# Edge stage of a graph network: padded operands, one compare, merged products, and an addition moved to POOL

## The chip, the cores and the metric

The kernel runs on one core of one Trainium2 chip. The metric is the device time of one execution in microseconds (us).

## What is computed

A block with three parts works on 6250 nodes of 256 features: a graph network over 200,000 edges, linear attention, and a mixture of eight experts. The change lies in the edges of the graph network alone. `g0` (64 scalars) and `g1` (64 vectors of 3) are the features of an edge's source node, `y0` and `y1` are four attributes of the edge, and `wa` to `wd` are weights that a small network makes from ten further attributes:

```python
h = silu(edge_length_embedded @ W_mlp1 / math.sqrt(N_BASIS))
ew = h @ W_mlp2 / math.sqrt(N_HID)
g0 = f0[edge_src]; g1 = f1[edge_src]
m0a = wa * g0 * y0[:, None]
m0b = wb * einsum('eum,em->eu', g1, y1) / math.sqrt(3.0)
m1a = wc[:, :, None] * g0[:, :, None] * y1[:, None, :]
m1b = wd[:, :, None] * g1 * y0[:, None, None]
s_mid = segment_sum(concatenate([m0a, m0b], 1), edge_dst)
v_mid = segment_sum(concatenate([m1a, m1b], 1), edge_dst)
```

The edges come sorted by destination.

## The kernel before

The program has six stages, one behind the other: `prepare`, `nodes`, `edges`, `update`, `dispatch` and `experts`. The stage of the change, `edges`, works through NI = 440 items. An item is a group of 512 edges (GE = 512, held as GC = 4 chunks of 128 edges, one edge per partition) seen against one block of 128 destination nodes. A group whose edges reach into a second block comes again as a further item. Each engine has a loop of its own over the items, unrolled four times, and semaphores tie the loops together. In the text, messages(n) stands for the messages of item n, and so on. For item n:

- SyncE (L657 to L671) waits until messages(n-4) and hot_y(n-4) are done (L661, L662; both counters start at FREE = 4), reads the group's number (L663), and issues six loads: `src`, `dst`, `y` (L665 to L667), and the ten edge attributes three times as high and low parts into 30 rows of `el` (L670).
- POOL (L673 to L683) waits for messages(n-4) and for the loads of n (L677, through `wait_apart`, L82), and then issues four indirect transfers (L679) that gather the 128 source rows of each chunk from a table in memory into `rows`.
- TensorE (L778 to L817) computes in `body`: `weights(n)`, the second layer of the small network in fp32 (L791); `hidden(n+1)`, its first layer with 30 rows against 512 columns (L785); and `sums(n-1)`, eight fp32 products (L802) that sum the messages by destination, with the one-hot matrices `hot_y` and `hot` as weights.
- ACT (L685 to L709) applies silu (L689), makes the vector part of `Z` from g0 and y1 in twelve activations (L696), and scales `hot` by y0 to `hot_y` in four (L703).
- DVE (L711 to L776) rebases the destinations (`rel`, L731), multiplies g1 by y1 (`dot3`, L736), compares with a ramp to get the one-hot matrices (`hot`, L742), adds two of the three parts of the dot product (`dot2`, L745) and later the third (L763, into the scalar part of `Z`), and multiplies `rows` and `Z` with the weights in four products (L754 and L758, each twice). The last of them, `scalars(1, Z[h])`, counts up `messages`. Then `flush(n-1)` (L724) adds the sums of the item before to the accumulators.

`src`, `dst`, `y`, `el` and `rows` have four buffers each; `rel`, `hot`, `hot_y`, `Z`, `dot3`, `dot2`, `msg`, `hT` and the PSUM tiles have two. No scheduler decides an order: every engine works through what its loop says, in that order.

## Time and profile before

| what | value |
|---|---|
| median of 3 runs | 3996.39 us (3994.59 to 3999.0) |
| span of the profiled execution | 3989.3 us |
| mean granted TensorE clock | 0.978 |
| busy: PE, DVE, ACT, POOL | 97%, 72%, 65%, 64% |
| edge stage, first gather to last flush | 274.47 to 2832.36 us |

The time of the profiled execution itself is not listed beside its span; the median of the runs is 7.1 us above the span. Busy time is work of an engine and leaves waits out. The same tile name `k_x` stands for everything that lies in the large buffer `K.x2` during this stage: `rows`, `Z`, `msg`, and, before the change, `dot3` and `dot2`. A gather is an instruction of POOL (about 1 us, in which its transfer is described) and a transfer that lands later.

### The profile page before, as it was taken

To read this page: it belongs to the slowest core of one execution; us is meant where nothing else is said; L and a number is where in the kernel's file an instruction comes from. 1 tells how busy PE (TensorE), PEld (TensorE's weight loads), DVE (VectorE), ACT (ScalarE), POOL (GpSimd) and SP (SyncE) were. 2 spreads that over 40 slices of the span, in tenths; PEclk is the share of its full clock that TensorE was granted. 3 is DMA by queue.
4 is the path that set the end of the run, shared out by engine and by line. 5 is a ranking of instruction groups with operands and counts; after the bars stand their busy time and mean duration, and the time that the engine had idled before them with its cause. 6 is when DMAs were issued, how large, how long until landed. Compare 5 with 4: busy or idle time off the path is not lost. (4 is left out here: it accounts for less than half of the span.)

```text
span 3989.3 us, 81744 instructions
## 1 busy us (share of the span) xinstructions
PE 3852.3 (97%) x18082; PEld 3206.0 (80%) x18082; DVE 2881.2 (72%) x5613; ACT 2595.5 (65%) x8731; POOL 2544.3 (64%) x2339
## 2 busy tenths in 40 slices
PE   6979999999999999999999999999997699999998
PEld 5868888888888888878887888788896588888887
DVE  7769999999999999999999999999666600000000
ACT  6668887888788778877887788778424233333332
POOL 5647777777777777777777777777311344444443
PEclk9989999999999999999999999999995899999999
DMA  7863333433333333434334334333222366666665
GB/s 224 257 194 103 102 103 103 104 103 104 103 104 103 104 103 104 104 103 104 104 103 104 103 104 104 104 103 104 75 79 87 104 186 194 193 193 193 194 193 151
DMA packets 436225, 509.01 MB, mean 128 GB/s; under 512 B 254375, under 2 KB 345355, under 8 KB 421851
## 3 DMA queue, kind: packets, MB, share of 16 engines
q0 software_dynamic: 109904, 273.02, 24.5%
q1 hardware_dynamic: 326283, 235.54, 20.7%
q8 instruction: 17, 0.28, 0.0%
q14 instruction: 21, 0.17, 0.0%
HBM read 444.92 MB, written 63.33 MB: 127 GB/s over the span
## 5 line engine op out<-in xcount | busy, mean ns | idle before, releaser
L679 POOL DMA_INDIRECT k_x<-gather_table,edges_src x1760 | 1996.8, 1135 | 557.4 <-issue 447.6
L696 ACT ACTIVATE k_x<-k_x,edges_y 128x64 f32<-128x64 f32 x5280 | 1303.5, 336 | 4.2 <-DMA k_x<-gather_table,edges_src 4.0
L802 PE MATMUL edges_ps_sum<-k_x,edges_hot_y 128*128 128x256 f32 x3520 | 1093.6, 392 | 0.5 <-issue 0.5
L802 PE MATMUL edges_ps_sum<-k_x,edges_hot 128*128 128x256 f32 x3520 | 1047.6, 379 | 0.0
L703 ACT ACTIVATE edges_hot_y<-edges_hot,edges_y 128x128 f32<-128x128 f32 x1760 | 562.7, 390 | 505.6 <-DVE edges_hot L742 505.6
L791 PE MATMUL edges_ps_edge<-k_w_e,edges_hT 100*128 100x256 f32 x3520 | 836.4, 380 | 7.8 <-ACT edges_hT L689 7.8
L758 DVE TENSOR_TENSOR k_x<-k_x,edges_ps_edge 128x768 f32<-128x768 f32 x880 | 794.6, 942 | 0.0
L802 PEld LDWEIGHTS edges_ps_sum<-k_x,edges_hot_y 128*128 128x128 f32 x3520 | 633.0, 190 | 175.5 <-issue 107.1
L791 PEld LDWEIGHTS edges_ps_edge<-k_w_e,edges_hT 100*128 100x128 f32 x3520 | 670.5, 191 | 101.7 <-issue 7.6
L802 PEld LDWEIGHTS edges_ps_sum<-k_x,edges_hot 128*128 128x128 f32 x3520 | 669.4, 190 | 91.3
L1407 DVE TENSOR_TENSOR experts_raw<-experts_ps_y,experts_b 128x256 f32<-128x256 f32 x112 | 42.4, 420 | 725.6 <-PE experts_ps_y L1363 725.6
L1317 POOL DMA_INDIRECT out<-experts_y,experts_idx_out x112 | 178.4, 1593 | 423.4 <-issue 386.6
L724 DVE TENSOR_TENSOR accumulators<-accumulators,edges_ps_sum 128x512 f32 x440 | 302.7, 688 | 171.7 <-PE edges_ps_sum L802 164.3
L736 DVE TENSOR_TENSOR k_x<-k_x,edges_y 128x768 f32<-128x768 f32 x440 | 419.4, 953 | 0.0
L1353 PE MATMUL experts_ps_h<-experts_xT,experts_w 128*128 128x256 f32 x1792 | 397.7, 380 | 1.7 <-ACT experts_xT L1381 1.6
L1363 PE MATMUL experts_ps_y<-experts_w,experts_hT 128*128 128x256 f32 x1792 | 396.0, 379 | 0.0
L1390 ACT ACTIVATE experts_hT<-experts_ps_h,experts_constants 128x256 f32<-128x256 f32 x448 | 212.5, 474 | 271.2 <-PE experts_ps_h L1353 271.2
L1353 PEld LDWEIGHTS experts_ps_h<-experts_xT,experts_w 128*128 128x128 f32 x1792 | 341.3, 191 | 49.5 <-ACT experts_xT L1381 1.9
L1363 PEld LDWEIGHTS experts_ps_y<-experts_w,experts_hT 128*128 128x128 f32 x1792 | 336.2, 190 | 43.4
L754 DVE TENSOR_TENSOR k_x<-k_x,edges_ps_edge 128x256 f32<-128x256 f32 x880 | 362.3, 412 | 1.6 <-PE edges_ps_edge L791 1.6
L742 DVE TENSOR_TENSOR edges_hot<-k_iota_f,edges_rel 128x512 f32<-128x512 f32 x440 | 301.3, 685 | 0.0
L1381 ACT ACTIVATE experts_xT<-experts_ps_x,experts_constants 128x256 f32<-128x256 f32 x112 | 57.2, 560 | 313.3 <-DMA experts_w<-in_w 313.3
(248 smaller groups left out, 3508.8 us busy)
## 6 DMA issues: line engine op xcount, KB each, us to landing
experts_w<-in_w SPq DMA_DIRECT2D x112, 1024.0 KB
k_x<-gather_table,edges_src POOLq DMA_INDIRECT x1760
edges_el<-el_hi SPq DMA_DIRECT2D x880, 20.0 KB
edges_el<-el_lo SPq DMA_DIRECT2D x440, 20.0 KB
nodes_el<-in_el SPq DMA_DIRECT2D x46, 170.0 KB, 3.6
el_hi<-nodes_el_hi SPq DMA_DIRECT2D x46, 170.0 KB
el_lo<-nodes_el_lo SPq DMA_DIRECT2D x46, 170.0 KB
experts_b<-in_b SPq DMA_DIRECT2D x56, 128.0 KB
```

The lines of the kernel that those rows point to most:

```text
L679: nc.gpsimd.indirect_dma_start(out=rows[k][:, j, :], out_offset=None, in_=K.table_d.rearrange("t p d -> (t p) d"), in_offset=bass.Indirect ...
L696: x = nc.scalar.activation(Z[k % 2][:, j, MUL * (i + 1):MUL * (i + 2)], rows[k][:, j, 0:MUL], ACT.Identity, scale=y[k][:, j, 1 + i:2 + i])
L703: x = nc.scalar.activation(hot_y[k % 2][:, j, :], hot[k % 2][:, j, :], ACT.Identity, scale=y[k][:, j, 0:1])
L724: v.tensor_tensor(a, a, ps_s[k % 2][:, :], ALU.add).then_inc(c["flushed"], 1)
L736: v.tensor_tensor(dot3[h][:, :, :, :], rows[k][:, :, MUL:D].rearrange("p c (i u) -> p c i u", i=3), y[k][:, :, 1:4].unsqueeze(3).to_broadc ...
L742: v.tensor_tensor(hot[h][:, :, :], K.iota_f[:, :].unsqueeze(1).to_broadcast([P, GC, P]), rel[h][:, :].unsqueeze(2).to_broadcast([P, GC, P] ...
L754: return v.tensor_tensor(msg[h][:, :, o * D:o * D + MUL], factor[:, :, 0:MUL], w[:, :, o * P:o * P + MUL], ALU.mult)
L758: return v.tensor_tensor(three(msg[h][:, :, o * D + MUL:(o + 1) * D]), three(factor[:, :, MUL:D]), spread(w[:, :, o * P + MUL:(o + 1) * P] ...
L791: x = t.matmul(ps_e[k % 2][:, j * 256:(j + 1) * 256], hT[k % 2][:, j * P:(j + 1) * P], K.w_e2[:, :], start=True, stop=True)
L802: x = t.matmul(into[:, :, o, :], rows_hot[k % 2][:, j, :], msg[k % 2][:, j, o * D:(o + 1) * D], start=j == 0 and o == 0, stop=j == GC - 1, ...
L1353: x = t.matmul(ps_h[j % 4][:, 0:SB], w1[k][:, h, j * P:(j + 1) * P], xT[k][:, h, :], start=h == 0, stop=h == 1)
L1363: x = t.matmul(ps_y[s][:, 0:D], hT[k][:, j, s * P:(s + 1) * P], w2[k][:, j, :], start=j == 0, stop=j == NH - 1)
```

## The change

All of it lies in `edges`, apart from the size and clearing of one weight tile:

- `el` gets 128 partitions instead of 30, cleared once by POOL, and `w_e1s` likewise (SyncE waits for the clearing before its first load). The hidden layer's matmul then has 128 rows, 98 of them zero.
- The rebasing and the compare become one instruction, which reads the integer destinations itself: (ramp + base) == dst. The ramp and `K.item_base` are as they were.
- `rows` and `Z` lie side by side in `both`, so that the four products become two: one of 8 x 192 columns for all vectors, and one of 8 x 64 for all scalars, which now comes last and counts up `messages`.
- `Z` and `hot` get four buffers; `dot3` and `dot2` get one, in the attention's weight tile, which is free in this stage.
- The last addition of the dot product (`third`) leaves DVE for POOL. POOL's loop for item n issues the gathers of item n and then `third(n-3)`. DVE waits for it (`dot`) ahead of the last product.
- DVE flushes item n-2 between `before(n)` and `after(n)`, where it flushed n-1 at the end of n.
- ACT's wait for messages ahead of `Z` is gone, and its wait ahead of `hot_y` goes by `summed`.

```diff
@@ prepare, POOL and DVE
+            g.memset(K.w_e1s[:, :].bitcast(f32), 0.0)
...
-            nc.vector.tensor_copy(K.w_e1s[:, :], w_part[:, :]).then_inc(scaled, 1)
+            nc.vector.tensor_copy(K.w_e1s[0:3 * BAS, :], w_part[:, :]).then_inc(scaled, 1)
@@ edges, buffers
-    FREE = 4
+    FREE, AHEAD = 4, 2
...
-        el, src, dst = four("el", [3 * BAS, GE], f32r), four("src", [P, GC], i32), four("dst", [P, GC], i32)
+        el, src, dst = four("el", [P, GE], f32r), four("src", [P, GC], i32), four("dst", [P, GC], i32)
...
+        both, msg = [cut(2 * k) for k in range(4)], [cut(8 + 2 * k) for k in range(2)]
+        rows, Z = ([b[:, :, o * D:(o + 1) * D] for b in both] for o in range(2))
@@ edges, SyncE
+            sp.wait_ge(c["padded"], 4)
+
             def body(n, k):

                 sp.wait_ge(c["messages"], n + 1)
@@ edges, POOL
+            for k in range(4):
+                nc.gpsimd.memset(el[k][:, :].bitcast(f32), 0.0).then_inc(c["padded"], 1)
+
             def body(n, k):

                 wait_apart(pool, c["passed"], (c["messages"], n + 1), (loaded[k], per(n, k, LD, 4)))
...
-            steps(pool, NI, 4, 0, body)
+                if not (isinstance(n, int) and n < 3):
+                    third(n - 3, (k - 3) % 4)
+
+            def third(n, k):
+                wait_apart(pool, c["passed"], (c["dot2"], n + 1))
+                nc.gpsimd.tensor_tensor(Z[k][:, :, 0:MUL], dot2[:, :, :], dot3[:, :, 2, :], ALU.add).then_inc(c["dot"], 1)
+            steps(pool, NI, 4, 4, body)
+            for n in range(NI - 3, NI):
+                third(n, n % 4)
@@ edges, ACT
-                act.wait_ge(c["messages"], n + 3)
...
-                act.wait_ge(c["flushed"], n + 1)
+                act.wait_ge(c["summed"], n + 1)
@@ edges, DVE
-                dve.wait_ge(c["hot"], n)
-                v.tensor_scalar(rel[h][:, :], dst[k][:, :], K.item_base[:, bass.ds(n, 1)], None,
-                                ALU.subtract).then_inc(c["rel"], 1)
+                dve.wait_ge(c["flushed"], n + 1)
+                v.scalar_tensor_tensor(hot[k][:, :, :], K.iota_f[:, :].unsqueeze(1).to_broadcast([P, GC, P]),
+                                       K.item_base[:, bass.ds(n, 1)], dst[k][:, :].unsqueeze(2).to_broadcast([P, GC, P]),
+                                       ALU.add, ALU.is_equal).then_inc(c["hot"], 1)
...
-                v.tensor_tensor(hot[h][:, :, :], K.iota_f[:, :].unsqueeze(1).to_broadcast([P, GC, P]),
-                                rel[h][:, :].unsqueeze(2).to_broadcast([P, GC, P]), ALU.is_equal).then_inc(c["hot"], 1)
...
-                v.tensor_tensor(Z[h][:, :, 0:MUL], dot2[h][:, :, :], dot3[h][:, :, 2, :], ALU.add).then_inc(c["dot"], 1)
-                vectors(0, rows[k])
                 dve.wait_ge(c["factors"], n + 1)
-                vectors(1, Z[h])
-                dve.wait_ge(c["dot"], n + 1)
-                scalars(1, Z[h]).then_inc(c["messages"], 1)
+                v.tensor_tensor(three(g[:, :, MUL:D]), three(f[:, :, MUL:D]),
+                                w[:, :, MUL:P].unsqueeze(2).to_broadcast([P, 2 * GC, 3, MUL]), ALU.mult)
+                dve.wait_ge(c["dot"], n + 1)
+                v.tensor_tensor(g[:, :, 0:MUL], f[:, :, 0:MUL], w[:, :, 0:MUL], ALU.mult).then_inc(c["messages"], 1)
...
+            def body(n, k):
+                before(n, k)
+                flush(n - 2, (k - 2) % 4)
+                after(n, k)
@@ edges, TensorE
-                pe.wait_ge(c["flushed"], n + 1)
+                pe.wait_ge(c["flushed"], n + 3)
```

The order of instructions on POOL, before the change, in the loop over the items (`L679 DMA` is a gather, the register and ISA rows are counters and waits):

```order
L56 ISA
L85 ISA
L679 DMA k_x<-gather_table,edges_src 128x256 x4
L85 REGISTER_ALU
L679 DMA k_x<-gather_table,edges_src 128x256 x4
L85 REGISTER_ALU
L679 DMA k_x<-gather_table,edges_src 128x256 x8
L56 REGISTER_ALU
L56 COMPARE_AND_BRANCH
```

And in the changed kernel, whose lines stand a few further down (L687 is the gather, L696 is `third`, whose operands `dot2` and `dot3` lie in `k_w_kvT`):

```order
L687 DMA k_x<-gather_table,edges_src 128x256 x4
L85 REGISTER_ALU
L696 TENSOR_TENSOR k_x<-k_w_kvT 128x4x64
L85 REGISTER_ALU
L687 DMA k_x<-gather_table,edges_src 128x256 x4
L85 REGISTER_ALU
L696 TENSOR_TENSOR k_x<-k_w_kvT 128x4x64
```

An addition now stands behind every four gathers; it belongs to the item three before the one that is gathered.

On DVE, before, one item from the rebasing to the last product:

```order
L731 TENSOR_SCALAR edges_rel<-edges_dst,k_item_base 128x4
L736 TENSOR_TENSOR k_x<-k_x,edges_y 128x4x192
L742 TENSOR_TENSOR edges_hot<-k_iota_f,edges_rel 128x512
L745 TENSOR_TENSOR k_x<-k_x 128x4x64
L754 TENSOR_TENSOR k_x<-k_x,edges_ps_edge 128x4x64
L762 REGISTER_ALU
L763 TENSOR_TENSOR k_x<-k_x 128x4x64
L758 TENSOR_TENSOR k_x<-k_x,edges_ps_edge 128x4x192 x2
L754 TENSOR_TENSOR k_x<-k_x,edges_ps_edge 128x4x64
```

And in the changed kernel (L745 is the compare, L739 the flush, L767 and L770 the merged products):

```order
L745 SCALAR_TENSOR_TENSOR edges_hot<-k_iota_f,k_item_base,edges_dst 128x512
L749 REGISTER_ALU
L751 TENSOR_TENSOR k_w_kvT<-k_x,edges_y 128x768
L735 REGISTER_ALU
L735 TENSOR_LOAD k_item_block
L735 ISA x2
L736 REGISTER_ALU
L739 ISA
L739 TENSOR_TENSOR accumulators<-accumulators,edges_ps_sum 128x512
L758 TENSOR_TENSOR k_w_kvT<-k_w_kvT 128x256
L767 TENSOR_TENSOR k_x<-k_x,edges_ps_edge 128x8x192
L770 TENSOR_TENSOR k_x<-k_x,edges_ps_edge 128x8x64
```

The flush moved up between the first product and the first addition, the second addition is gone from DVE, and the product that completes the messages is the last instruction of the item as before.

## Rows read from the trace of the kernel before

**Rows 1.** The page, part 1: busy us (share of the span) and instructions.

```profile
PE 3852.3 (97%) x18082; PEld 3206.0 (80%) x18082; DVE 2881.2 (72%) x5613; ACT 2595.5 (65%) x8731; POOL 2544.3 (64%) x2339
```

**Rows 2.** A stretch: us, busy of PE, PEld, DVE, ACT, POOL, clock, DMA share, GB/s.

```profile
1100.00:1600.00 500.00, 500.00 (x2164) 400.69 (x2163) 467.57 (x867) 399.46 (x1470) 393.84 (x347) 1.00 0.40 104
```

**Rows 3.** Order of time on PE, one item: start us, duration us, engine, line.

```profile
1504.09 1.89 PE L791 MATMUL edges_ps_edge<-k_w_e,edges_hT 100*128 100x256 f32 x8
1505.91 0.47 PE L785 MATMUL edges_ps_hidden<-edges_el,k_w_e1s 30*100 30x512 f32 x1
1506.32 0.70 PE L802 MATMUL edges_ps_sum<-k_x,edges_hot_y 128*128 128x256 f32 x2
1506.85 0.59 PE L802 MATMUL edges_ps_sum<-k_x,edges_hot 128*128 128x256 f32 x2
...
1509.87 1.89 PE L791 MATMUL edges_ps_edge<-k_w_e,edges_hT 100*128 100x256 f32 x8
```

**Rows 4.** Order of time on DVE, one item; in brackets idle time before.

```profile
1503.68 0.41 DVE L754 TENSOR_TENSOR k_x<-k_x,edges_ps_edge 128x256 f32<-128x256 f32 x1
1504.47 0.69 DVE L724 TENSOR_TENSOR accumulators<-accumulators,edges_ps_sum 128x512 f32 x1 [0.38 <-PE edges_ps_sum L802]
...
1505.21 0.95 DVE L736 TENSOR_TENSOR k_x<-k_x,edges_y 128x768 f32<-128x768 f32 x1
1506.08 0.69 DVE L742 TENSOR_TENSOR edges_hot<-k_iota_f,edges_rel 128x512 f32<-128x512 f32 x1
1506.68 0.42 DVE L745 TENSOR_TENSOR k_x<-k_x 128x256 f32<-128x256 f32 x1
...
1507.72 1.81 DVE L758 TENSOR_TENSOR k_x<-k_x,edges_ps_edge 128x768 f32<-128x768 f32 x2
```

**Rows 5.** Order of time on POOL, one item.

```profile
1505.51 1.53 POOL L679 DMA_INDIRECT k_x<-gather_table,edges_src  x1 [0.30 <-issue]
1507.35 1.01 POOL L679 DMA_INDIRECT k_x<-gather_table,edges_src  x1 [0.30 <-DMA edges_el<-el_lo]
```

**Rows 6.** Waits of SyncE: queue and line, waited for, us in total, times, longest.

```profile
SPq L663 <- DVE k_x L754: 750.2, 436, 2.4
```

**Rows 7.** Order of time on SyncE: the first load of an item.

```profile
1505.19 0.36 SPq L665 DMA_DIRECT2D edges_src<-in_src  x1
```

**Rows 8.** Start of the edge stage on SyncE.

```profile
269.63 0.35 SPq L665 DMA_DIRECT2D edges_src<-in_src  x1
```

**Rows 9.** Start of the edge stage on POOL.

```profile
274.47 1.07 POOL L679 DMA_INDIRECT k_x<-gather_table,edges_src  x1 [11.35 <-DMA edges_el<-el_hi]
...
278.48 1.01 POOL L679 DMA_INDIRECT k_x<-gather_table,edges_src  x1 [0.30 <-issue]
```

**Rows 10.** Order of time on POOL in the node stage.

```profile
131.18 1.01 POOL L398 DMA_INDIRECT nodes_dst<-in_dst_rows,first_groups_i  x1 [0.30 <-issue]
132.21 0.74 POOL L420 TENSOR_TENSOR nodes_q<-nodes_q_high,nodes_q_low 128x256 f32<-128x256 f32 x1
```

**Rows 11.** PE at the stage's start, with the granted clock at 0.50.

```profile
286.57 3.78 PE L791 MATMUL edges_ps_edge<-k_w_e,edges_hT 100*128 100x256 f32 x8 [0.69 <-ACT edges_hT L689]
290.29 0.74 PE L785 MATMUL edges_ps_hidden<-edges_el,k_w_e1s 30*100 30x512 f32 x1
290.96 1.22 PE L802 MATMUL edges_ps_sum<-k_x,edges_hot_y 128*128 128x256 f32 x2
291.97 1.06 PE L802 MATMUL edges_ps_sum<-k_x,edges_hot 128*128 128x256 f32 x2
```

**Rows 12.** The same stretch: us, busy of each engine, clock.

```profile
285.00:294.00 9.00, 8.31 (x18) 5.51 (x18) 7.57 (x14) 5.82 (x21) 7.06 (x7) 0.50 0.39 105
```

**Rows 13.** A memset of POOL (groups by line: busy us, mean ns).

```profile
L160 POOL MEMSET k_zeros<- 128x512 f32 x1 | 0.5, 537 | 0.0
```

**Rows 14.** DVE: end of the first item, and the last flush.

```profile
287.65 0.41 DVE L754 TENSOR_TENSOR k_x<-k_x,edges_ps_edge 128x256 f32<-128x256 f32 x1
...
2831.67 0.69 DVE L724 TENSOR_TENSOR accumulators<-accumulators,edges_ps_sum 128x512 f32 x1 [3.41 <-PE edges_ps_sum L802]
```

More of the change, by code:

```diff
@@ L638, in edges @@
         two = lambda name, shape, dt=f32: [m.sb(f"{name}{k}", shape, dt) for k in range(2)]
-        el, src, dst = four("el", [3 * BAS, GE], f32r), four("src", [P, GC], i32), four("dst", [P, GC], i32)
-        y = four("y", [P, GC, 4])
-        rel, hT = two("rel", [P, GC]), two("hT", [HID, GE])
-        hot, hot_y = two("hot", [P, GC, P]), two("hot_y", [P, GC, P])
+        el, src, dst = four("el", [P, GE], f32r), four("src", [P, GC], i32), four("dst", [P, GC], i32)
+        y, hT = four("y", [P, GC, 4]), two("hT", [HID, GE])
+        hot, hot_y = four("hot", [P, GC, P]), two("hot_y", [P, GC, P])
+        spare = K.w_kvT[:, :, :].rearrange("p c n -> p (c n)")
+        dot3 = spare[:, 0:3 * GC * MUL].rearrange("p (c i u) -> p c i u", c=GC, i=3)
+        dot2 = spare[:, 3 * GC * MUL:].rearrange("p (c u) -> p c u", c=GC)
         warm = m.sb("warm", [P, 1])
         room = K.x2[:, :, :].rearrange("p t d -> p (t d)")
-        cut = lambda at, n: room[:, at * GC * D:(at + n) * GC * D].rearrange("p (c n) -> p c n", c=GC)
-        rows, Z, msg = [cut(k, 1) for k in range(4)], [cut(4 + k, 1) for k in range(2)], [cut(6 + 2 * k, 2) for k in range(2)]
-        dot3 = [cut(10 + k, 1)[:, :, 0:3 * MUL].rearrange("p c (i u) -> p c i u", i=3) for k in range(2)]
-        dot2 = [cut(10 + k, 1)[:, :, 3 * MUL:] for k in range(2)]
+        cut = lambda at: room[:, at * GC * D:(at + 2) * GC * D].rearrange("p (c n) -> p c n", c=GC)
+        both, msg = [cut(2 * k) for k in range(4)], [cut(8 + 2 * k) for k in range(2)]
+        rows, Z = ([b[:, :, o * D:(o + 1) * D] for b in both] for o in range(2))
         ps_e = [m.ps(f"edge{k}", 2) for k in range(2)]
@@ L651, in edges @@
         loaded, gathered = ([m.sem(f"{x}{k}") for k in range(4)] for x in ("loaded", "gathered"))
-        c = {x: m.sem(x) for x in ("cleared", "messages", "flushed", "hidden", "act", "weights", "factors", "rel", "hot_y",
+        c = {x: m.sem(x) for x in ("padded", "cleared", "messages", "flushed", "hidden", "act", "weights", "factors", "hot_y",
                                    "dot3", "dot2", "dot", "hot", "summed", "passed")}
@@ L692, in body @@
                 act.wait_ge(gathered[k], per(n, k, 64, 4))
-                act.wait_ge(c["messages"], n + 3)
                 for j in range(GC):
                     for i in range(3):
-                        x = nc.scalar.activation(Z[k % 2][:, j, MUL * (i + 1):MUL * (i + 2)], rows[k][:, j, 0:MUL],
+                        x = nc.scalar.activation(Z[k][:, j, MUL * (i + 1):MUL * (i + 2)], rows[k][:, j, 0:MUL],
                                                  ACT.Identity, scale=y[k][:, j, 1 + i:2 + i])
@@ L700, in body @@
                 act.wait_ge(c["hot"], n + 1)
-                act.wait_ge(c["flushed"], n + 1)
+                act.wait_ge(c["summed"], n + 1)
                 for j in range(GC):
-                    x = nc.scalar.activation(hot_y[k % 2][:, j, :], hot[k % 2][:, j, :], ACT.Identity, scale=y[k][:, j, 0:1])
+                    x = nc.scalar.activation(hot_y[k % 2][:, j, :], hot[k][:, j, :], ACT.Identity, scale=y[k][:, j, 0:1])
                 x.then_inc(c["hot_y"], 1)
@@ L746, in body @@
                                 ALU.add).then_inc(c["dot2"], 1)
+                eight = lambda a: a.rearrange("p c (o n) -> p (c o) n", o=2)
+                w = ps_e[h][:, :].rearrange("p (g n) -> p g n", g=2 * GC)
+                three = lambda a: a.rearrange("p g (i u) -> p g i u", i=3)
+                f, g = eight(both[k]), eight(msg[h])
                 dve.wait_ge(c["weights"], n + 1)
-                w = ps_e[h][:, :].rearrange("p (c n) -> p c n", c=GC)
-                three = lambda a: a.rearrange("p c (i u) -> p c i u", i=3)
@@ L751, in body @@
-                spread = lambda a: a.unsqueeze(2).to_broadcast([P, GC, 3, MUL])
-                def scalars(o, factor):
-                    return v.tensor_tensor(msg[h][:, :, o * D:o * D + MUL], factor[:, :, 0:MUL],
-                                           w[:, :, o * P:o * P + MUL], ALU.mult)
-                def vectors(o, factor):
-                    return v.tensor_tensor(three(msg[h][:, :, o * D + MUL:(o + 1) * D]), three(factor[:, :, MUL:D]),
-                                           spread(w[:, :, o * P + MUL:(o + 1) * P]), ALU.mult)
@@ L778, in _ @@
+            for n in range(2):
+                before(n, n)
+                after(n, n)
+            steps_from(dve, 2, NI, 4, body)
+            for n in (NI - 2, NI - 1):
+                flush(n, n % 4)
         @block.tensor
@@ L800, in sums @@
                 for j in range(GC):
-                    for o, rows_hot in ((0, hot_y), (1, hot)):
-                        x = t.matmul(into[:, :, o, :], rows_hot[k % 2][:, j, :], msg[k % 2][:, j, o * D:(o + 1) * D],
+                    for o, rows_hot in ((0, hot_y[k % 2]), (1, hot[k])):
+                        x = t.matmul(into[:, :, o, :], rows_hot[:, j, :], msg[k % 2][:, j, o * D:(o + 1) * D],
                                      start=j == 0 and o == 0, stop=j == GC - 1, skip_group_check=True)
```

29 lines of the change are left out of this document (10 added, 19 removed).

## The prediction

> **What bounds the kernel now.** I read the busy shares first, then the stretches, then one item of the edge stage on each engine, then its start. TensorE is busy 97% of the span [rows 1], and in the middle of the edge stage 500.00 us of 500 at the full clock (1.00, which is the 2.4 GHz level) [rows 2]. An item takes 5.78 us there: the first weight-network product starts at 1504.09 and the next item's at 1509.87 [rows 3]. So TensorE sets the pace, and its 440 items, 5.78 each, are some 2540 us of the 3989.
>
> The other engines have room. DVE waits 0.38 us for the sums before each flush and works for the other 5.40 [rows 4]. POOL starts four gathers per item 1.31 us apart, 5.25 us in all, and the last 0.53 of its period is a gather that lasts 1.53 instead of 1.01 [rows 5]. The loads have slack of another kind, which matters below. SyncE waits at L663, 436 times, for the DVE product L754 that completes an item's messages [rows 6]. That product ends at 1503.68 + 0.41 = 1504.09, and the first load of item n+4 is issued at 1505.19 [rows 4, 7]. What then follows (loads, gathers, the item's work) may take four items, 23.1 us, since there are four buffers. A long latency is hidden by this depth, and a part of the chain that loses the depth would show it in full.
>
> **The change, part by part.**
>
> *DVE.* It loses the rebasing (L731), one addition (L763) and the start-up of two merged products. From the end of one item's messages to the wait for `dot` it has the compare (0.69), the product (0.95), the flush (0.69), the first addition (0.42) and the vectors' product (1.81) [rows 4]: 4.6 us at most. Whatever the merged forms and the integer operand of the compare cost (between nothing and a doubling of the compare, 0.69) lies under the wait that I find next, which leaves DVE idle for some 7 us.
>
> *TensorE.* Padding the hidden layer from 30 to 128 rows leaves 512 columns. Today the hidden layer costs 0.41 us from its start to the next matmul, the product behind it 0.53 where the seven others take (1509.87 - 1506.85) / 7 = 0.43 each, and the four products ahead of it 1.82 where four times 0.43 is 1.73 [rows 3]. (A product of 256 columns in fp32 shows as two records, x2.) The part that padding could remove is between nothing and 0.41 + 0.10 + 0.09 - 0.22 = 0.38 us, with 0.22, one record's share of 0.43, as the least that a matmul here takes. The Trainium skill (TensorE: Matmul & The Clock Gate, Step-by-step: what each phase is for) says that loading weights takes time by columns and that the number of rows does not matter; by that the padding would give nothing, unless its other statement, that a load is only pulled ahead when row groups do not conflict, is what the 30-row tile runs into. The sum below does not depend on it.
>
> *POOL.* This is the term that decides. The addition that completes Z (L763) moves to POOL as `third(n-3)`, and it stands there behind the four gathers of item n. POOL works in order. Those gathers wait for the loads of item n, and SyncE issues these only when the messages of item n-4 are done. Shift the index by one and follow it round: messages(n-1) are complete; SyncE may load item n+3; POOL may gather item n+3; only then comes `third(n)`; only then can DVE make the last product of item n, which completes messages(n). The step from one item's messages to the next now contains a whole load, four gathers, the addition and a product. The four-deep buffers no longer help, because the chain passes from n-1 to n, not from n-4 to n. Its price:
>
> - messages to the first load's issue: 1505.19 - 1504.09 = 1.10 us [rows 4, 7];
> - first issue to the start of the first gather: at the stage's start, where POOL was waiting, 274.47 - 269.63 = 4.84 us [rows 8, 9]. With gathers of the item before still in flight it can be longer. Bounds: 4.5, and 5.8 (one microsecond more). I take 5.0, near the row;
> - four gathers with POOL otherwise idle: from 274.47 to 278.48 + 1.01 = 279.49, that is 5.02 us [rows 9];
> - the addition behind a gather: the same form starts 0.02 us after a gather's end and takes 0.74 [rows 10]; with 0.05 for the semaphore (an estimate; ACT's and SyncE's starts behind DVE's ends are of this size) 0.81 us;
> - the last product, now 128x512 from PSUM: the flush of that size takes 0.69 [rows 4].
>
> Together 1.10 + 5.00 + 5.02 + 0.81 + 0.69 = 12.62 us per item, where 5.78 was. Bounds 12.1 to 13.4.
>
> Does anything else reach that length? DVE's other work, 4.6 us, does not. ACT's does not: it fits in 5.78 today. TensorE is now busy for 5.4 to 5.8 us in 12.6, and its clock may fall. When it was at 0.50, the 1.2 GHz level, the second layer's four products took 290.29 - 286.57 = 3.72, the hidden layer 0.67, and the first of the sums 1.01; seven more at twice 0.43 make 11.4 us per item [rows 11, 12]. That is still under 12.62, and it runs beside the chain: sums(n-1), weights(n+1) and hidden(n+2) all lie between messages(n-1) and messages(n). So the clock costs nothing, with about a microsecond to spare.
>
> *How many items.* Loads 4 to 439 wait for messages 0 to 435, and each then holds back the addition three items behind: messages 1 to 436, so 436 rounds: 436 x 12.62 = 5502 us.
>
> *Ends of the stage.* Before the first load POOL now clears four 128x512 tiles, 4 x 0.54 [rows 13] = 2.1 us. messages(0) then need all sixteen first gathers: 274.47 + 2.1 + 15 x 1.31 + 1.01, some 0.8 for collisions with DVE, the addition 0.81 and the product 0.69 give 299.6; before, they were done at 288.06 [rows 14]. Behind messages(436) three items remain without loads, some 15 us, then the last sums (8 x 0.43 = 3.5) and a flush (0.7): 19 us. The stage ends at 299.6 + 5502 + 19 = 5820.6 instead of 2831.67 + 0.69 = 2832.4 [rows 14]. Nothing behind it changes. The difference is +2988 us on the profiled span of 3989.3. The median of the runs, 3996.4, lies 7.1 above that span, and I keep this distance: 3996.4 + 2988 = 6984, say **6985 us**.
>
> **The rivals.**
>
> *1. TensorE stays the bound (ends faster).* If POOL's order did not hold the addition back, the stage would keep TensorE's pace and win what padding gives, 0 to 0.38 us x 440 = 0 to 167 us: 3830 to 3996, middle 3915. For it: TensorE has no gap at all today, and the four engines' busy times all fit in 5.8 us. Against it: it needs the load of item n+3 to be issued before messages(n-1), and SyncE is seen to wait exactly there [rows 6]; or the addition to overtake gathers. It decides for this rival only if the round costs less than 5.8 us, and the four gathers and the addition alone are 5.8. Chance 3%.
>
> *2. POOL's own work becomes the bound, without the round.* Four gathers at 1.31, the addition 0.76, and collisions. The long gather shows what these are: it starts at 1505.51, inside DVE's product of two SBUF operands (L736, from 1505.21, next start 1506.08), and lasts 1.53 instead of 1.01; 1506.08 is also where the extra 0.52 ends [rows 4, 5]. The addition reads two SBUF operands and could be held up the same way, and hold up DVE. With one or two such losses POOL needs 6.2 to 6.9 us per item: (6.5 - 5.78) x 440 = +320, so 4315 us. The Trainium skill (SBUF — State Buffer, SBUF: two separate sides) calls this an exclusive lock between GpSimd and a DVE operation with two SBUF inputs; the trace agrees, by the 0.52. Against this rival: DVE is idle while POOL gathers and adds in the round, so the two would seldom meet. Chance 2%.
>
> *3. The round without the load.* If loads were early and only the gathers' wait for messages mattered, the round would be 0.9 + 5.02 + 0.81 + 0.69 = 7.4 us, (7.4 - 5.78) x 436 = +707: 4700 us. Against it stands SyncE's wait again. Chance 2%.
>
> *4. The round, and TensorE's low clock as the bound.* If at 1.2 GHz an item costs over 12.6 us (11.4 from the rows, plus waits of its own order), the stage goes by TensorE: at 13.5 us per item +3370, so 7365 us. It decides from 1.2 us more than the rows show. Chance 3%.
>
> **How the numbers follow.** The forecast has the remaining 90%. Its time is 6985. Its own range comes from the round's bounds: 12.1 gives 436 x 0.52 = 227 less, and 13.4 gives 340 more. 6800 to 7300 holds most of that (some nine parts in ten), about 81% of all; the rivals are left out. A measurement of this kernel can tell 0.2% (8 us) from no change. Rival 1's 3% splits into faster, 2%, and within 0.2%, 1%, where padding gives next to nothing; slower has 97%.
>
> **What would show it.** In the changed profile, one item should take about 12.6 us in the middle of the edge stage, and TensorE's busy share there should fall to 45% at full clock or up to 90% at half. The wait that ends DVE's scalar product should be POOL's addition. POOL should be idle for about 6 us per item, released by a load of `edges_el`, then run four gathers and the addition without a gap. SyncE's wait for DVE's messages should be far more than half of its time. If one item takes 6 to 7 us, rival 2 or 3 was right; if TensorE shows no idle time, rival 1 or 4. If DVE shows more than 5 us of work per item, the compare with an integer operand is dearer than I bound it, without effect on the time.

## The result and the profile after

| | before | changed |
|---|---|---|
| median of 4 runs | 3996.95 us | 6861.47 us (6859.99 to 6865.73) |
| ratio, 95% interval | 1 | 1.7171 (1.7147 to 1.7196) |
| profiled span | 3989.3 us | 6859.2 us |
| mean granted TensorE clock | 0.978 | 0.811 |

The forecast was 6985 us, within 6800 to 7300. Some 2865 us went into the edge stage and nowhere else of note. Part 1 of the page of the changed kernel, and two of its groups (busy us, mean ns, idle time of the engine before them and who ended it):

```profile
PE 4754.9 (69%) x18082; PEld 3888.0 (57%) x18082; DVE 2623.3 (38%) x3853; ACT 2595.5 (38%) x8731; POOL 2659.9 (39%) x2784
...
L770 DVE TENSOR_TENSOR k_x<-k_x,edges_ps_edge 128x512 f32<-128x512 f32 x440 | 302.6, 688 | 3286.7 <-POOL k_x L696 3286.7
...
L745 DVE SCALAR_TENSOR_TENSOR edges_hot<-k_iota_f,k_item_base,edges_dst 128x512 f32<-128x512 f32 x440 | 328.2, 746 | 0.0
```

No engine is near its limit any more. The last product of an item, L770, has 3286.7 us of idle time before it, all of it ended by POOL's L696, the addition that moved. In the middle of the stage (us, busy of PE, PEld, DVE, ACT, POOL, clock, DMA share, GB/s) the stretch that answers to [rows 2] is:

```profile
3000.00:3500.00 500.00, 317.52 (x1013) 250.65 (x1014) 197.40 (x246) 188.94 (x695) 192.14 (x201) 0.77 0.18 48
```

TensorE, which had no gap before, is busy for 317.52 of 500 us, at a mean clock of 0.77.

One round can be followed over three engines. First POOL in order of time (start us, duration us, in brackets the idle time and its releaser), which answers to [rows 5]:

```profile
2999.72 0.73 POOL L696 TENSOR_TENSOR k_x<-k_w_kvT 128x256 f32<-128x256 f32 x1
3007.01 1.03 POOL L687 DMA_INDIRECT k_x<-gather_table,edges_src  x1 [6.56 <-DMA edges_el<-el_hi]
...
3010.97 1.01 POOL L687 DMA_INDIRECT k_x<-gather_table,edges_src  x1 [0.30 <-issue]
3012.00 0.74 POOL L696 TENSOR_TENSOR k_x<-k_w_kvT 128x256 f32<-128x256 f32 x1
```

POOL's wait behind 2999.72 ends with the last of six loads. SyncE's first load in the same stretch, [rows 7]:

```profile
3002.15 0.36 SPq L670 DMA_DIRECT2D edges_src<-in_src  x1
```

And the wait of SyncE with the largest total in the whole run (us in total, times, longest), [rows 6]:

```profile
SPq L668 <- DVE k_x L770: 3677.2, 436, 11.4
```

DVE in the same stretch, [rows 4]:

```profile
3000.48 0.69 DVE L770 TENSOR_TENSOR k_x<-k_x,edges_ps_edge 128x512 f32<-128x512 f32 x1 [7.53 <-POOL k_x L696]
3001.09 0.74 DVE L745 SCALAR_TENSOR_TENSOR edges_hot<-k_iota_f,k_item_base,edges_dst 128x512 f32<-128x512 f32 x1
3001.75 0.95 DVE L751 TENSOR_TENSOR k_w_kvT<-k_x,edges_y 128x768 f32<-128x768 f32 x1
3002.62 0.68 DVE L739 TENSOR_TENSOR accumulators<-accumulators,edges_ps_sum 128x512 f32 x1
3003.21 0.41 DVE L758 TENSOR_TENSOR k_w_kvT<-k_w_kvT 128x256 f32<-128x256 f32 x1
3003.55 1.74 DVE L767 TENSOR_TENSOR k_x<-k_x,edges_ps_edge 128x1536 f32<-128x1536 f32 x1
3012.78 0.69 DVE L770 TENSOR_TENSOR k_x<-k_x,edges_ps_edge 128x512 f32<-128x512 f32 x1 [7.49 <-POOL k_x L696]
```

Read in order: the messages of one item are done at 3000.48 + 0.69 = 3001.17. SyncE, which waited for just that, issues the next loads from 3002.15. They release POOL's gathers at 3007.01, after 6.56 us of idle time. Behind the fourth gather comes the addition, at 3012.00. Its end at 3012.74 releases DVE's last product at 3012.78, and the next item is done 12.30 us after the first. DVE had finished the rest of that item's work at 3005.29 and stood idle for 7.49 us. SyncE's wait for DVE grew from 750.2 to 3677.2 us, in the same 436 times; that is two thirds of the stage. Over the whole run POOL waits 437 times for a load ahead of a gather, and DVE 437 times for POOL's addition.

| term of the round | forecast | measured |
|---|---|---|
| messages to the first load's issue | 1.10 | 3002.15 - 3001.17 = 0.98 |
| first issue to the first gather | 5.00 | 3007.01 - 3002.15 = 4.86 |
| four gathers | 5.02 | 3011.98 - 3007.01 = 4.97 |
| the addition and its semaphore | 0.81 | 3012.78 - 3011.98 = 0.80 |
| the last product | 0.69 | 0.69 |
| sum | 12.62 | 12.30 |

The ends of the stage, [rows 14], on DVE: the first item's last product, then that of item 436, the last whose addition stood behind a load, and the last flush.

```profile
300.80 0.69 DVE L770 TENSOR_TENSOR k_x<-k_x,edges_ps_edge 128x512 f32<-128x512 f32 x1 [10.10 <-POOL k_x L696]
```

```profile
5676.18 0.69 DVE L770 TENSOR_TENSOR k_x<-k_x,edges_ps_edge 128x512 f32<-128x512 f32 x1 [7.41 <-POOL k_x L696]
...
5696.46 0.69 DVE L739 TENSOR_TENSOR accumulators<-accumulators,edges_ps_sum 128x512 f32 x1 [2.77 <-PE edges_ps_sum L808]
```

The first messages are done at 301.49 (forecast 299.6), those of item 436 at 5676.87, and the stage ends at 5697.15. That makes (5676.87 - 301.49) / 436 = 12.33 us for a round on average, and 20.3 us for the tail (forecast 19).

TensorE's low clock, [rows 11], in the same round as above:

```profile
3001.27 1.19 PE L808 MATMUL edges_ps_sum<-k_x,edges_hot_y 128*128 128x256 f32 x2 [4.29 <-issue]
3002.25 1.06 PE L808 MATMUL edges_ps_sum<-k_x,edges_hot 128*128 128x256 f32 x2
...
3007.85 1.89 PE L797 MATMUL edges_ps_edge<-k_w_e,edges_hT 100*128 100x256 f32 x8
```

The sums start at 3001.27, behind 4.29 us of idle time, and a product takes 0.85 to 0.86 us from start to start, twice the 0.43 of before: that is the 1.2 GHz level (half of 2.4). Partway through this item the clock rises again: the second layer, four products, takes 1.89 us as before. The engine is done with everything that it can do at about 3010 and waits some 3.6 us for the next messages. The clock costs nothing here.

The tail shows what the padding is worth. The last three items are held up by no load, and TensorE runs without a gap ([rows 3] before):

```profile
5682.03 1.89 PE L797 MATMUL edges_ps_edge<-k_w_e,edges_hT 100*128 100x256 f32 x8
5683.57 0.58 PE L791 MATMUL edges_ps_hidden<-edges_el,k_w_e1s 128*100 128x512 f32 x1
5684.00 0.59 PE L808 MATMUL edges_ps_sum<-k_x,edges_hot_y 128*128 128x256 f32 x2
...
5687.45 1.89 PE L797 MATMUL edges_ps_edge<-k_w_e,edges_hT 100*128 100x256 f32 x8
5689.18 0.60 PE L808 MATMUL edges_ps_sum<-k_x,edges_hot_y 128*128 128x256 f32 x2
```

The second layer takes 1.54 us to the hidden layer's start (1.82 before), the hidden layer 0.43 to the sums (0.41 before), and the first of the sums 0.43 (0.53 before). An item takes 5687.45 - 5682.03 = 5.42 us, 0.36 less than before. In the last item no hidden layer stands between the second layer and the sums, and the second layer takes 5689.18 - 5687.45 = 1.73 us. So the hidden layer costs 1.54 + 0.43 - 1.73 = 0.24 us in all, where it cost 1.82 + 0.41 + 0.10 - 1.73 = 0.60.

The rows of the weight loads (PEld) show where this comes from. Before, in the item of [rows 3]:

```profile
1505.91 0.16 PEld L785 LDWEIGHTS edges_ps_hidden<-edges_el,k_w_e1s 30*100 30x100 f32 x1 [0.33 <-issue]
1506.31 0.30 PEld L802 LDWEIGHTS edges_ps_sum<-k_x,edges_hot_y 128*128 128x128 f32 x2 [0.24 <-issue]
```

And changed, in the tail:

```profile
5683.55 0.17 PEld L791 LDWEIGHTS edges_ps_hidden<-edges_el,k_w_e1s 128*100 128x100 f32 x1
5683.76 0.42 PEld L808 LDWEIGHTS edges_ps_sum<-k_x,edges_hot_y 128*128 128x128 f32 x2
```

Before, 0.33 and 0.24 us of idle time stand ahead of the two loads, and the load for the sums starts with its product (1506.31 and 1506.32). With 128 rows each load follows the one before without such idle time, and the load for the sums starts 0.24 us ahead of its product at 5684.00.

### The profile page after: what moved, and what is told of

Same layout as the page of the kernel before. It is cut to its first block and busy times, and to the rows that moved or that the text cites. A ratio compares the mean times of both kernels' runs of the same rounds, so it can differ in the third digit from the quotient of the medians.

```text
span 6859.2 us, 80530 instructions
## 1 busy us (share of the span) xinstructions
PE 4754.9 (69%) x18082; PEld 3888.0 (57%) x18082; DVE 2623.3 (38%) x3853; ACT 2595.5 (38%) x8731; POOL 2659.9 (39%) x2784
## 5 line engine op out<-in xcount | busy, mean ns | idle before, releaser
L687 POOL DMA_INDIRECT k_x<-gather_table,edges_src x1760 | 1786.2, 1015 | 3286.0 <-DMA edges_el<-el_hi 2848.8
L808 PE MATMUL edges_ps_sum<-k_x,edges_hot_y 128*128 128x256 f32 x3520 | 1661.2, 569 | 1963.7 <-DVE k_x L770 1449.8
L808 PEld LDWEIGHTS edges_ps_sum<-k_x,edges_hot_y 128*128 128x128 f32 x3520 | 975.9, 291 | 2344.9 <-DVE k_x L770 1594.0
L770 DVE TENSOR_TENSOR k_x<-k_x,edges_ps_edge 128x512 f32<-128x512 f32 x440 | 302.6, 688 | 3286.7 <-POOL k_x L696 3286.7
L808 PE MATMUL edges_ps_sum<-k_x,edges_hot 128*128 128x256 f32 x3520 | 1509.6, 523 | 0.0
L808 PEld LDWEIGHTS edges_ps_sum<-k_x,edges_hot 128*128 128x128 f32 x3520 | 999.4, 284 | 240.2
L767 DVE TENSOR_TENSOR k_x<-k_x,edges_ps_edge 128x1536 f32<-128x1536 f32 x440 | 767.8, 1745 | 2.2 <-ACT k_x L711 1.7
L751 DVE TENSOR_TENSOR k_w_kvT<-k_x,edges_y 128x768 f32<-128x768 f32 x440 | 418.3, 951 | 0.5 <-DMA k_x<-gather_table,edges_src 0.5
L696 POOL TENSOR_TENSOR k_x<-k_w_kvT 128x256 f32<-128x256 f32 x440 | 322.9, 734 | 21.8 <-DVE k_w_kvT L758 11.4
L745 DVE SCALAR_TENSOR_TENSOR edges_hot<-k_iota_f,k_item_base,edges_dst 128x512 f32<-128x512 f32 x440 | 328.2, 746 | 0.0
L739 DVE TENSOR_TENSOR accumulators<-accumulators,edges_ps_sum 128x512 f32 x440 | 299.1, 680 | 4.0 <-PE edges_ps_sum L808 4.0
```

The source lines that it names most:

```text
L687: nc.gpsimd.indirect_dma_start(out=rows[k][:, j, :], out_offset=None, in_=K.table_d.rearrange("t p d -> (t p) d"), in_offset=bass.Indirect ...
L696: nc.gpsimd.tensor_tensor(Z[k][:, :, 0:MUL], dot2[:, :, :], dot3[:, :, 2, :], ALU.add).then_inc(c["dot"], 1)
L745: v.scalar_tensor_tensor(hot[k][:, :, :], K.iota_f[:, :].unsqueeze(1).to_broadcast([P, GC, P]), K.item_base[:, bass.ds(n, 1)], dst[k][:, : ...
L751: v.tensor_tensor(dot3[:, :, :, :], rows[k][:, :, MUL:D].rearrange("p c (i u) -> p c i u", i=3), y[k][:, :, 1:4].unsqueeze(3).to_broadcast ...
L767: v.tensor_tensor(three(g[:, :, MUL:D]), three(f[:, :, MUL:D]), w[:, :, MUL:P].unsqueeze(2).to_broadcast([P, 2 * GC, 3, MUL]), ALU.mult)
L770: v.tensor_tensor(g[:, :, 0:MUL], f[:, :, 0:MUL], w[:, :, 0:MUL], ALU.mult).then_inc(c["messages"], 1)
```

## The experiments

Twelve runs were made, in four groups, each with the kernel before measured beside it. One thing has to be said ahead of them. In the first three groups the kernel before itself took 4679 to 4693 us (medians of 7 runs), and in the fourth 3995.05. The second group and the fourth ran on the same chip, so it isn't a matter of the chip. A ratio within a group is fair, but it holds for the disturbed condition, and times of the first three groups aren't to be held against 3996. What went slow there is read further down. It cost the kernel before some 700 us; by the traces the kernels with the addition on DVE and with the padding alone suffered likewise, and the others little or not at all.

**The addition back on DVE.**

```diff
@@ edges, POOL
-                if not (isinstance(n, int) and n < 3):
-                    third(n - 3, (k - 3) % 4)
...
@@ edges, DVE, after the vectors' product
+                dve.wait_ge(c["dot2"], n + 1)
+                v.tensor_tensor(Z[k][:, :, 0:MUL], dot2[:, :, :], dot3[:, :, 2, :], ALU.add).then_inc(c["dot"], 1)
```

> The changed kernel with the last addition put back on DVE, behind the vectors' product; padding, one compare and merged products stay. Theory (the round through the load, four gathers and the addition on POOL makes all of the slowdown): the round is gone, TensorE is the bound again and keeps what padding gives. In the changed kernel's tail, where no load stands in the way, an item took 5687.45 - 5682.03 = 5.42 us on TensorE, 0.36 less than before, so 440 x 0.36 = 158 us less than before: about 3840 us. Rival (the merged products, the compare or the single dot3 buffer cost time of their own): between 3900 and 4200. Rival (TensorE's clock fell for another reason than its waits): it stays slow, above 5000.

Measured: 4520.24 us where the kernel before took 4693.37, ratio 0.9643 (0.9614 to 0.9671). Two more runs of the same kernel:

> The same kernel as e1_add_on_dve, once more, since in that call the kernel before itself took 4693 us instead of 3996. Theory (no round, TensorE the bound, padding's 0.36 us kept): about 3840 us where the kernel before takes 3996, a ratio of 0.96. Rival (merged products or compare cost time): ratio 0.98 to 1.05.

Measured: 4511.56 against 4679.19, ratio 0.9672 (0.9589 to 0.9756).

> e1_add_on_dve a third time, beside e9 on the same chip. Theory: 3840 us if the kernel before takes 3996 here, a ratio of 0.961; 0.965 if it takes 4690 as in the calls before.

Measured: 4515.26 against 4678.70, ratio 0.9627 (0.9597 to 0.9658).

The ratio is near what the theory gave, 0.96, in all three; its time, 3840 us, wasn't seen, because the kernel before wasn't at 3996 in any of these groups. The ratio by itself proves little, since both of its times hold some 700 us that the theory knows nothing of. The traces say more: in the middle of the stage (600 to 2600 us) 34 to 38% of the items take 5.40 to 5.43 us from one second layer to the next on TensorE, and next to none the 5.78 of before. That is TensorE's pace with the padding. For the main question this is enough: with the addition on DVE, and all else of the change in place, the slowdown of 1.72 is gone and a gain of 3 to 4% is left in the disturbed groups. So none of the other parts (padding, compare, merged products, single `dot3`) carries the loss.

**The padding alone.** The kernel before, with the larger and cleared `el` and `w_e1s` and nothing else.

```diff
-        el, src, dst = four("el", [3 * BAS, GE], f32r), four("src", [P, GC], i32), four("dst", [P, GC], i32)
+        el, src, dst = four("el", [P, GE], f32r), four("src", [P, GC], i32), four("dst", [P, GC], i32)
...
-        K.w_e1s = sb("w_e1s", [3 * BAS, HID], f32r)
+        K.w_e1s = sb("w_e1s", [P, HID], f32r)
```

> The kernel before with nothing but the padded el and w_e1s tiles. Theory (the 30-row weights were loaded late and kept TensorE waiting on both sides of the hidden layer; 128 rows end that): 0.36 us per item, 3840 us. Rival (rows don't matter, the 0.36 in the changed kernel's tail comes from somewhere else): 3996 us. If DVE, which works 5.40 of 5.78 us, then sets the pace, the gain is cut to 0.2 to 0.3 us per item, 3870 to 3910 us.

Measured: 4638.95 against 4693.37 us, ratio 0.9903 (0.9867 to 0.9940).

> The same kernel as e2_padding_alone, once more for the same reason. Theory: 0.36 us per item less, 3840 us, or 3870 to 3910 us if DVE with its 5.40 us of work then sets the pace. Rival (padding gives nothing): 3996 us.

Measured: 4592.84 against 4679.19, ratio 0.9843 (0.9759 to 0.9927).

A gain is there, but at 54 and 86 us it is smaller than was expected. In the trace of the first of the two, items that nothing held up look like this on TensorE:

```profile
623.74 1.89 PE L797 MATMUL edges_ps_edge<-k_w_e,edges_hT 100*128 100x256 f32 x8
625.28 0.58 PE L791 MATMUL edges_ps_hidden<-edges_el,k_w_e1s 128*100 128x512 f32 x1
...
629.15 1.89 PE L797 MATMUL edges_ps_edge<-k_w_e,edges_hT 100*128 100x256 f32 x8
630.70 0.58 PE L791 MATMUL edges_ps_hidden<-edges_el,k_w_e1s 128*100 128x512 f32 x1
```

629.15 - 623.74 = 5.41 us per item instead of 5.78, and the hidden layer starts 1.54 us behind the second layer instead of 1.82. So the padding by itself takes the 0.36 us away where nothing else holds the item up, in 26 to 29% of the items; the rival that rows don't matter is out. How much of it the whole kernel would keep where it takes 3996 wasn't measured.

**A seventh load.** One more load of `dst` per item on SyncE, into a tile that nobody reads. POOL waits for it with the others.

```diff
+                sp.dma_start(more[k][:, :], one(A["dst"])).then_inc(loaded[k], 16)
```

> The changed kernel with a seventh load per item on SyncE (dst once more, 2 KB, into a tile that nobody reads), which POOL waits for with the others. Theory: a load's issue lies in the round, so an item takes 0.46 us more (0.38 and the 0.08 between two issues), 436 x 0.46 = 200 us: 7060 us. Rival (loads are hidden by the four buffers, something else is the round): 6860 us as without it.

Measured: 7049.24 us, that is 188 more than the changed kernel's 6861, where 200 was expected and the rival gave nothing. A load's issue lies in the round: its average length in the trace is 12.75 us where it was 12.33. In this group the kernel before took 4693 us, and yet the time came out near what was worked out from undisturbed traces.

**The load taken out of the round.** SyncE waits for `dot3` instead of `messages`. Together with `hot_y` that covers every reader of the four loaded tiles.

```diff
-                sp.wait_ge(c["messages"], n + 1)
+                sp.wait_ge(c["dot3"], n + 1)
                 sp.wait_ge(c["hot_y"], n + 1)
...
+            dve.sem_inc(c["dot3"], FREE)
...
-                dve.wait_ge(c["dot3"], n + 1)
+                dve.wait_ge(c["dot3"], n + 1 + FREE)
```

> The changed kernel, but SyncE waits for dot3 and hot_y of item n-4 instead of messages(n-4) and hot_y(n-4), before it loads item n. All readers of the four loaded tiles are done by then. Theory: the load leaves the round, which is now POOL's wait for messages, a restart of 0.9, four gathers 5.02, the addition 0.78 and the product 0.69: 7.4 to 7.7 us per item (rival 3's number), 4700 to 4850 us. Rival (the gathers alone, or DVE's wait, make the 12.3 us): stays above 6500 us.

Measured: 4928.97 us. That is 1932 us less than the changed kernel, and 79 above the upper end of what was expected. POOL and DVE in order of time:

```profile
1504.37 0.73 POOL L696 TENSOR_TENSOR k_x<-k_w_kvT 128x256 f32<-128x256 f32 x1
1506.78 1.48 POOL L687 DMA_INDIRECT k_x<-gather_table,edges_src  x1 [1.68 <-DVE k_x L771]
1508.56 1.01 POOL L687 DMA_INDIRECT k_x<-gather_table,edges_src  x1 [0.30 <-DVE k_w_kvT L759]
```

```profile
1505.14 0.69 DVE L771 TENSOR_TENSOR k_x<-k_x,edges_ps_edge 128x512 f32<-128x512 f32 x1 [3.04 <-POOL k_x L696]
...
1506.40 0.95 DVE L752 TENSOR_TENSOR k_w_kvT<-k_x,edges_y 128x768 f32<-128x768 f32 x1
```

The messages are done at 1505.14 + 0.69 = 1505.83, POOL's gathers start at 1506.78, and one round is 1506.78 less the 1498.87 at which the gathers of the round before started, 7.9 us. The messages come 7.85 us apart in most rounds. The first gather lasts 1.48 instead of 1.01 (1.53 in many other rounds): it starts inside DVE's product of two SBUF operands (1506.40), as in [rows 5]. The expectation had left out this 0.47, which is 0.47 x 436 = 205 us, more than the miss.

**The addition two items behind, and one.** `third(n-2)` and `third(n-1)` in place of `third(n-3)`; the numbers 3 in POOL's loop become 2 or 1.

```diff
-                if not (isinstance(n, int) and n < 3):
-                    third(n - 3, (k - 3) % 4)
+                if not (isinstance(n, int) and n < 1):
+                    third(n - 1, (k - 1) % 4)
...
-            for n in range(NI - 3, NI):
+            for n in range(NI - 1, NI):
```

> The changed kernel with third(n-2) behind the gathers of item n instead of third(n-3). Theory: the round now leads from messages(n-2) to messages(n), so the same 12.3 us are shared by two items, 6.15 us each, and POOL's own work (four gathers at 1.31 and the addition 0.76, 6.0 us) is just below; collisions with DVE may add up to 0.5: 6.15 to 6.6 us per item, 4160 to 4360 us. Rival (the slowdown comes from POOL's addition as such, its lock on SBUF against DVE, not from its place): stays near 6860 us.

Measured: 4399.68 us, 2462 less than with three behind and 40 above the upper end of what was expected. In the trace half of the messages come 6.52 to 6.54 us apart, and the average is 6.69.

> The changed kernel with third(n-1) behind the gathers of item n. Theory: a round of 12.3 us is shared by three items, 4.1 us each, so it is no bound; POOL's own work is, four gathers at 1.31 and the addition 0.76, 6.0 us, and about 0.5 of collisions with DVE: 6.1 to 6.6 us per item, 4150 to 4360 us. Rival (third(n-1) comes too late behind the landing of the next gathers): over 7 us per item, above 4550 us.

Measured: 4319.99 us, within what was expected. Both were in disturbed groups. For the second, POOL and DVE in order of time:

```profile
1502.33 1.02 POOL L687 DMA_INDIRECT k_x<-gather_table,edges_src  x1 [0.16 <-issue]
1503.65 1.65 POOL L687 DMA_INDIRECT k_x<-gather_table,edges_src  x1 [0.30 <-issue]
1505.60 1.01 POOL L687 DMA_INDIRECT k_x<-gather_table,edges_src  x1 [0.30 <-DVE k_w_kvT L758]
1506.91 1.01 POOL L687 DMA_INDIRECT k_x<-gather_table,edges_src  x1 [0.30 <-issue]
1507.95 0.73 POOL L696 TENSOR_TENSOR k_x<-k_w_kvT 128x256 f32<-128x256 f32 x1
1508.84 1.03 POOL L687 DMA_INDIRECT k_x<-gather_table,edges_src  x1 [0.16 <-issue]
```

```profile
1502.81 0.74 DVE L745 SCALAR_TENSOR_TENSOR edges_hot<-k_iota_f,k_item_base,edges_dst 128x512 f32<-128x512 f32 x1
1503.47 0.95 DVE L751 TENSOR_TENSOR k_w_kvT<-k_x,edges_y 128x768 f32<-128x768 f32 x1
```

POOL has no idle time left: from 1502.33 to 1508.84 there are four gathers, the addition, and only the short gaps that it always has. One item takes 6.51 us, of which 0.64 is the gather of 1.65 instead of 1.01, which starts while DVE's product with two SBUF operands (1503.47) is in progress. The messages come 6.51 to 6.55 us apart throughout. This is the price that rival 2 had forecast (6.5 us per item, 4315 us), and it comes about once the round is out of the way. So the place of one instruction decides between two bounds: three items behind, the round, 12.3; one or two behind, POOL's own work, 6.5. What a round shared by two or three items would take (6.15 and 4.1 us by the expectations) lies below POOL's own work and wasn't seen.

**Earlier loads on top of the addition on DVE.** The edits of both kernels above together.

> e1_add_on_dve with SyncE's wait of e7_load_early (dot3 instead of messages), so that loads can start some 3 us earlier in an item. In the two calls before, the kernel before took about 4690 us instead of 3996, SyncE's load instructions were broken up and late, and engines waited for loads. Theory: where SyncE is late, the head start of the loads wins it back, most of the 700 us; where SyncE is not late, TensorE is the bound and the time is that of e1_add_on_dve, 3840 us. Rival (the pauses are not a matter of late loads): the same ratio to the kernel before as e1_add_on_dve, 0.965.

Measured: 4481.68 against 4678.70 us, ratio 0.9593 (0.9549 to 0.9637), beside 0.9627 for the same kernel without the early loads. The theory falls. The head start won back 34 us of about 700, not most of them, and the intervals of the two ratios overlap. In the disturbed groups the fastest version relative to the kernel before is another one, the addition on POOL one item behind: 4319.99 against 4679.19 us, ratio 0.9252 (0.9149 to 0.9355). Held against 3996 it would be the slower kernel.

**Both kernels again.**

> The kernel before, unchanged, for a trace of it where it takes about 4690 us. Theory: SyncE's issue of loads is held up while POOL gathers, the loads come late, and DVE, ACT and TensorE wait for them in some of the items, while most items still take 5.8 us or less; the node and expert stages take what they took. Rival (a slower memory or clock in general): every item is longer by the same part, and the expert stage too.

Measured: 3996.64 us. The disturbance was gone, so no disturbed trace of the kernel before exists, and the expectation is untested.

> The changed kernel, unchanged, beside it. Theory: its loads are issued while POOL is idle and its gathers run while SyncE is idle, so nothing holds up the loads: 6861 us as before, 12.3 us per item. Rival (slower memory or clock in general): over 7500 us.

Measured: 6861.97 us, beside 3995.05 for the kernel before. The time is the expected one, but nothing was disturbed in this group, so it doesn't show whether a disturbance would leave this kernel alone.

What the traces show of the disturbance is this. The first of SyncE's six loads, by its smallest, median and largest duration in ns, first in the undisturbed trace of the kernel before:

```profile
L665 SPq DMA_DIRECT2D edges_src<-in_src x346: 361/363/365, 600.5 to 2594.6; - x173
```

and in the disturbed trace of the kernel with the addition on DVE:

```profile
L670 SPq DMA_DIRECT2D edges_src<-in_src x286: 3/361/728, 604.6 to 2598.3; - x143
```

Half of SyncE's load instructions there are recorded with a duration under 0.25 or over 0.45 us, where all lie between in the undisturbed trace. The loads come late by it: from the start of the first of an item's six loads to the end of the last it is 2.66 to 2.69 us in every item of the kernel before, and in the disturbed kernel 2.67 us or less in a quarter of the items, 3.1 in the median and 9.4 at most. POOL and TensorE wait longer (us in total, times, longest, from 600 to 2600 us), first the undisturbed kernel before:

```profile
POOL k_x L679 <- issue: 346.7, 1128, 0.7
```

and the disturbed kernel, whose second line the kernel before doesn't have:

```profile
POOL k_x L687 <- issue: 618.1, 1040, 6.4
PEld edges_ps_edge L791 <- issue: 228.6, 75, 8.9
```

What lies behind the edge stage is unhurt: it takes 1161 us in this trace and 1157 in the undisturbed one. In the expert stage TensorE is busy for all of 700 us at full clock, with 192 GB/s moved (193 in the undisturbed trace of the kernel before, 3270 to 3970 us).

```profile
3800.00:4500.00 700.00, 700.00 (x3340) 616.42 (x3339) 67.24 (x196) 235.79 (x491) 278.41 (x291) 1.00 0.63 192
```

In the kernel with a seventh load, SyncE issues its loads while POOL is idle, and there every load took its usual time in a disturbed group. In all the others of these three groups some loads were recorded shorter or longer, but not all of them suffered: where the addition is one or two items behind on POOL, or the loads are early on top of the changed kernel, an item's six loads never took more than 3.8 us, and only the six traces with the addition on DVE or the padding alone have items with 6.9 to 9.4. That is a pattern, not a cause. What brought the disturbance on and took it away again stays open.

## Why the prediction was right

**The round.** The step on which it all rested was: "The step from one item's messages to the next now contains a whole load, four gathers, the addition and a product." The trace shows each link in that order, each releasing the next, and the waits counted over the run (436 of SyncE, 437 of POOL, 437 of DVE) say that it is so in every round. Three experiments priced it from different sides: one load more made it 0.42 us longer per item (188 us over 436 rounds gives 0.43); without the load it was 7.9 us instead of 12.3; and with the addition off POOL it was gone. That the distance of three items is what closes the round is shown by the two kernels with two and one.

**The sizes.** The sum was 124 us too high, and nearly all of that is in the round's length: 12.62 against 12.33 on average, 0.29 x 436 = 126 us. The two terms that were highest above the measured ones were the issue behind the messages (1.10, measured 0.98) and the load (5.00, chosen above the row's 4.84 for gathers in flight, measured 4.86). The first was read from one item; the next item in the same trace has its messages at 1509.86 and its load at 1510.84, and gives 0.98. For the second the row itself would have been nearer: in the round no gather is being described while the loads are issued. What is left of the difference cancels, and that is luck: the first messages came 1.9 us later than forecast, the tail was 1.3 longer and what follows the stage 5 us longer, while the median lies only 2.3 us above the profiled span instead of 7.1.

**TensorE's clock.** It was said to cost nothing even at 1.2 GHz for a whole item. The granted clock in fact went up and down within items, 0.77 on average in the stretch from 3000 us, and the engine was busy for 64% of that stretch; it was done some 3.6 us before the next sums could start. Rival 4 had no part.

**DVE.** The compare with an integer operand takes 0.746 us where the old one took 0.685, and the merged vector product 1.745 where two took 1.81. All of it was hidden under the wait for POOL, as was said.

**Padding.** The bounds for it were 0 to 0.38 us; it is 0.36, at the upper end. The sum behind the upper bound holds as a whole and not in its parts. The hidden layer's cost in all fell from 0.60 to 0.24 us, close to the 0.22 that was taken as the least. But the second layer's part was put at 0.09, and the hidden layer now starts 0.28 us sooner behind it, while the hidden layer's own 0.41 became 0.43. Of the two statements of the Trainium skill that the prediction named (TensorE: Matmul & The Clock Gate, Step-by-step: what each phase is for), the one on columns and rows would have had the padding give nothing, and the time of a load agrees with it: 0.16 us with 30 rows, 0.17 with 128. The saving lies in when the loads start, and the other statement is about that. But it says that a load is pulled ahead when the row groups don't conflict, or when it goes to the background weight buffer. The trace agrees in so far as the loads now come sooner. It doesn't bear out row groups as the reason, since both the 30 rows and the 128 share rows with the 100-row and 128-row products beside them, and it is with the larger tile that the loads come sooner. The reason stays open. In the changed kernel none of the saving could show ahead of the tail, since TensorE was no longer the bound.

**The rivals.** None of them is what the changed kernel does, but each priced another kernel. Rival 1's range for a kernel without the round (ratio 0.96 to 1) holds what the addition on DVE gives, 0.963 to 0.967, though only in disturbed groups. Rival 3 forecast 7.4 us and was 0.47 short, for the collision that only rival 2 had in it. Rival 2's 6.5 us, the middle of its 6.2 to 6.9, is what the addition one item behind takes.

## What to carry to other kernels

When an instruction is moved to another engine's queue, look at what stands ahead of it there and at what that work waits for. If the work ahead waits for the result of the instruction, be it by way of a buffer that comes free some items earlier, there is a round, and its period is the sum of its links divided by the number of items that it spans. Four buffers hide a latency of four items only as long as no link behind them shortens the way to one item: with a look-ahead of d items and four buffers, 4 - d items share the round. The period was measured for d = 3 alone. At d = 2 and 1 the runs show that the full round no longer bounds the kernel, and not how long the shared one is.

## What the runs showed that was not expected

- The same program can take 17% longer (4679 to 4693 us instead of 3995) in one group of runs than in another, on the same chip, with all that lies behind the edge stage unhurt. SyncE's loads come late where they overlap POOL's gathers. A kernel in which the two alternate, the one with a seventh load, didn't feel it (7049 us); the changed kernel itself was never run in a disturbed group. Two kernels in which they overlap, with the addition one and two items behind, hardly felt it either.
- Loads that are issued earlier didn't cure it: 34 us of some 700.
- A gather of POOL that starts while DVE runs the product of 768 columns with two SBUF operands takes longer by what is left of that product, and then its usual 1.01 us: 0.47 us more in one kernel, 0.64 in another, 0.52 before. In the kernel before, the some 200 such gathers from 700 to 1900 us take from 1.60 us, when they start 0.24 us into the product, down to 1.22, when they start 0.61 us into it. Gathers that start beside DVE's products with a PSUM operand keep their 1.01. In the kernel before, POOL's slack takes it up; in a kernel bound by POOL or by the round it comes once per item and costs 200 to 280 us.
